# The bias keys' dot products with the query weights, moved from GpSimd and VectorE to TensorE

## What is computed

```python
qh = (q_in @ wq + bq).reshape(b, q_len, H, K)
kh = (kv_in @ wk + bk).reshape(b, t, H, K)
kh = jnp.concatenate([kh, jnp.broadcast_to(bias_k, (b, 1, H, K))], axis=1)
logits = jnp.einsum('bqhk,bthk->bhqt', qh, kh) / scale
```

## Time and profile before

| what | us |
|---|---|
| median of 3 runs | 1135.85 (1135.51 to 1137.48) |
| the profiled execution's own time | 1132.89 |
| its span in the trace | 1131.1 |
| TensorE matmul busy | 956.8 (85%) |
| TensorE weight loads busy | 809.0 (72%) |
| VectorE busy | 817.2 (72%) |
| ScalarE busy | 603.5 (53%) |
| GpSimd busy | 336.1 (30%) |
| mean granted TensorE clock | 0.929 of full |

### The profile page before, as it was taken

The page is one execution under the profiler, slowest core; times in us unless marked ns, Lnnn a source line. Parts: engine busy times, 40 slices in busy tenths (PEclk is TensorE's granted clock), DMA queues, the critical chain, the costliest instruction groups (busy, mean ns, idle before and its releaser), DMA issues. The chain is left out here.

```text
span 1131.1 us, 17854 instructions
## 1 busy us (share of the span) xinstructions
PE 956.8 (85%) x6548; PEld 809.0 (72%) x6548; DVE 817.2 (72%) x1624; ACT 603.5 (53%) x1367; POOL 336.1 (30%) x325
## 2 busy tenths in 40 slices
PE   4888886569999999997899999998586898478958
PEld 3666665558888889887778989987475566465647
DVE  3377767976787878787578787877664787757865
ACT  2488873034555555553355555655424786257842
POOL 4255541441112222221111222200005454534520
PEclk8889997888999999998899999999788799688989
DMA  5984106140001111111000111000305930296120
GB/s 180 252 130 63 12 1 247 56 162 1 15 24 38 38 39 38 38 38 39 1 4 36 38 38 38 2 1 1 117 1 123 169 44 1 59 191 73 13 80 19
DMA packets 37810, 69.49 MB, mean 61 GB/s; under 512 B 7414, under 2 KB 23288, under 8 KB 35036
## 3 DMA queue, kind: packets, MB, share of 16 engines
q1 hardware_dynamic: 37724, 68.35, 24.7%
HBM read 57.31 MB, written 11.02 MB: 60 GB/s over the span
## 5 line engine op out<-in xcount | busy, mean ns | idle before, releaser
L1230 ACT CAST L1a_probsT_hi<-L1a_bank 128x512 fp32r<-128x512 f32 x128 | 68.8, 589 | 94.3 <-PE L1a_bank L1111 94.3
L1069 POOL TENSOR_SCALAR L1a_wo_hi<-L1a_stage 128x512 fp32r<-128x512 f32 x16 | 10.3, 646 | 363.2 <-PE L1a_sums L74 355.6
L1347 DVE TENSOR_REDUCE L1a_top<-L1a_scores 128x2 f32<-128x1024 f32 x64 | 78.2, 1222 | 36.1 <-PE L1a_scores L74 36.1
L1262 ACT ACTIVATE L1a_probs<-L1a_scores,L1a_neg_max 128x512 f32<-128x512 f32 x128 | 86.8, 684 | 30.6 <-DVE L1a_bias_shifted L1351 25.6
L1285 DVE TENSOR_TENSOR L1a_probsT_lo<-L1a_bank,L1a_probsT_hi 128x512 fp32r<-128x512 f32 x128 | 82.0, 682 | 0.1
L72 PE MATMUL L1a_bank<-L1a_probsT_hi,L1a_v_hi 128*128 128x256 f32 x256 | 73.2, 286 | 9.2 <-DVE L1a_probsT_lo L1285 9.2
L1232 ACT ACTIVATE L1a_attended_hi<-L1a_bank,L1a_cols 128x256 fp32r<-128x256 f32 x64 | 30.5, 476 | 90.4 <-PE L1a_bank L74 90.4
L72 PE MATMUL L1a_bank<-L1a_w_hi,ctxT_hi 128*128 128x256 f32 x256 | 76.5, 299 | 1.1 <-DVE latT_lo L1303 1.0
L74 PE MATMUL L1a_bank<-L1a_w_hi,ctxT_lo 128*128 128x256 f32 x256 | 73.7, 288 | 0.0
L73 PE MATMUL L1a_bank<-L1a_w_lo,ctxT_hi 128*128 128x256 f32 x256 | 73.6, 288 | 0.0
L390 POOL TENSOR_SCALAR L0a_probs<-L0a_probs,L0a_inverse 128x768 f32<-128x768 f32 x64 | 57.2, 906 | 52.9 <-DVE L0a_inverse L641 52.9
(11 more groups left out here) (409 smaller groups left out, 3160.8 us busy)
## 6 DMA issues: line engine op xcount, KB each, us to landing
L1a_stage<-in_L_w SPq DMA_DIRECT2D x15, 1024.0 KB, 4.8
L0m_fold_wq<-in_L_wq SPq DMA_DIRECT2D x2, 2048.0 KB, 19.8
L0a_k_stack<-L0a_k_dram SPq DMA_DIRECT2D x12, 192.0 KB
L0a_w_qkv<-L0a_k_dram SPq DMA_DIRECT2D x12, 192.0 KB
L0a_probs<-in_L_wo SPq DMA_DIRECT2D x1, 2048.0 KB, 9.7
L0a_probsT<-in_L_wo SPq DMA_DIRECT2D x1, 2048.0 KB, 11.2
L0m_stage<-in_L_wm SPq DMA_DIRECT2D x4, 512.0 KB, 5.8
L0m_fold_bias_k<-in_L_bias_k SPq DMA_DIRECT2D x2, 1024.0 KB, 15.4
```

What stands on the lines that cost most here:

```text
L1230: nc.scalar.copy(out, source).then_inc(ring.hi_done, 1)
L1262: nc.scalar.activation(probs[:, g % 2, qt, :], scores[:, qt, :], ACT.Exp, bias=neg_max[:, g % 2, qt:qt + 1], accum_out=row_sum[:, g % 2, q ...
L1347: link(nc.vector.tensor_reduce(top[:, :], scores[:, :, :], AX.X, ALU.max))
```

## The change

GpSimd's three multiplies, VectorE's one and its four reductions are gone, and so is the broadcast load of `bias_k`. The query weights are now handed in transposed, `L1_wqT` [128, 16, 256]: the 128 columns of a head lie on the partitions. In their place TensorE makes 64 fp32 matmuls, one for each attention, half of the 256 input rows, and head: the stationary side is a 128 x 128 piece of the transposed weights, the moving side one column, the head's `bias_k` (from `L1_cols`, 32 KB, loaded in place of the broadcast). Each gives one column of a bank. This is one more job of the ring, `fold_job`, between the last up job and the first down job; the down jobs take the next bank each. ScalarE copies the 128 x 64 result to `folded`.

```diff
--- before.py
+++ after.py
@@ -777,7 +777,8 @@
         w2 = [t[:, 4:8, :].rearrange("p s (g n) -> p (s g) n", g=2) for t in w]
         rows = keep[cfg["rows"]]
         up0 = KT
-        down0 = up0 + FT + (len(context.jobs) if cfg["context"] else 0)
+        fold_job = up0 + FT
+        down0 = up0 + FT + (len(context.jobs) if cfg["context"] else 0) + (1 if fold else 0)
 
         @block.sync
         def _(sp):
@@ -800,8 +801,6 @@
         @block.gpsimd
         def _(pool):
             parts.root(nc, pool)
-            if fold:
-                fold.multiply(nc, pool, nc.gpsimd, fold.pieces[:3])
             if cfg["context"]:
                 context.root(nc, pool)
 
@@ -821,6 +820,9 @@
                 last.then_inc(ring.full, 1)
             if cfg["context"]:
                 context.transpose(nc, pe, ring, keep)
+            if fold:
+                ring.wait_bank(pe, fold_job)
+                fold.multiply(nc, pe, ring.bank(fold_job)).then_inc(ring.full, 1)
             pe.wait_ge(w_lo, 8)
             for t in range(RT):
                 job = down0 + t
@@ -850,6 +852,10 @@
                                      bias=b1[:, m:m + 1]).then_inc(ring.hi_done, 1)
             if cfg["context"]:
                 context.scale(nc, act, ring)
+            if fold:
+                act.wait_ge(ring.full, fold_job + 1)
+                nc.scalar.copy(keep["folded"][:, :, :, :].rearrange("p i k h -> p (i k h)"),
+                               ring.bank(fold_job)[:, 0:2 * KT * H]).then_inc(ring.freed_by(fold_job), 1)
 
         @block.vector
         def _(dve):
@@ -874,17 +880,11 @@
                     context_link = Chain(dve, context.dve_done)
                     dve.wait_ge(context_loaded, 16)
                     context.statistics(nc, context_link, context_rows, 1e-5, True)
-                if fold and m >= FT - 2:
-                    fold.reduce(nc, dve, keep, *fold.pieces[m - FT + 2])
                 if cfg["context"] and m == 3:
                     context.apply(nc, dve, context_rows, True)
             if cfg["context"]:
                 context.split(nc, dve, context_link, ring, cfg["context"])
-            if fold:
-                fold.multiply(nc, dve, nc.vector, fold.pieces[3:])
             for t in range(RT):
-                if fold and t < 2:
-                    fold.reduce(nc, dve, keep, *fold.pieces[3 - t])
                 job = down0 + t
                 dve.wait_ge(ring.full, job + 1)
                 nc.vector.tensor_tensor(keep["x"][:, t, :], ring.bank(job)[:, 0:D], keep["x"][:, t, :],
@@ -895,29 +895,26 @@
 
 
 
+
     def __init__(self, ph):
-        self.wq = [ph.sb(f"fold_wq{i}", [P, KT, H * DW]) for i in range(2)]
-        self.bias_k = [ph.sb(f"fold_bias_k{i}", [P, H * DW]) for i in range(2)]
+        self.wq = [ph.sb(f"fold_wq{i}", [P, H, D]) for i in range(2)]
+        self.cols = [ph.sb(f"fold_cols{i}", [P, 4, H]) for i in range(2)]
         self.loaded = [ph.sem(f"fold_loaded{i}") for i in range(2)]
-        self.multiplied = [[ph.sem(f"fold_multiplied{i}{kt}") for kt in range(KT)] for i in range(2)]
-        self.pieces = [(i, kt) for i in range(2) for kt in range(KT)]
 
     def load(self, sp, io):
         for i in range(2):
-            sp.dma_start(self.bias_k[i][:, :], io[f"L1_bias_k{i + 1}"].partition_broadcast(P)).then_inc(self.loaded[i], 16)
-            sp.dma_start(self.wq[i][:, :, :], io[f"L1_wq{i + 1}"].rearrange("(k p) n -> p k n", p=P)).then_inc(self.loaded[i], 16)
-
-    def multiply(self, nc, engine, on, pieces):
-
-        for i, kt in pieces:
-            engine.wait_ge(self.loaded[i], 32)
-            on.tensor_tensor(self.wq[i][:, kt, :], self.wq[i][:, kt, :], self.bias_k[i][:, :],
-                             ALU.mult).then_inc(self.multiplied[i][kt], 1)
-
-    def reduce(self, nc, dve, keep, i, kt):
-        dve.wait_ge(self.multiplied[i][kt], 1)
-        nc.vector.tensor_reduce(keep["folded"][:, i, kt, :], self.wq[i][:, kt, :].rearrange("p (h d) -> p h d", h=H),
-                                AX.X, ALU.add)
+            sp.dma_start(self.cols[i][:, :, :], io[f"L1_cols{i + 1}"]).then_inc(self.loaded[i], 16)
+            sp.dma_start(self.wq[i][:, :, :], io[f"L1_wqT{i + 1}"]).then_inc(self.loaded[i], 16)
+
+    def multiply(self, nc, pe, bank):
+        for i in range(2):
+            pe.wait_ge(self.loaded[i], 32)
+            for kt in range(KT):
+                for h in range(H):
+                    at = (i * KT + kt) * H + h
+                    last = nc.tensor.matmul(bank[:, at:at + 1], self.wq[i][:, h, kt * P:(kt + 1) * P],
+                                            self.cols[i][:, 1, h:h + 1], start=True, stop=True)
+        return last
 
 
 def wide_attentions(nc, io, keep):
@@ -1460,7 +1457,7 @@
         by_pair = [tiles(w).reshape(P, KT, PAIRS, 2 * DW).transpose(2, 0, 1, 3).reshape(PAIRS, P, -1) for w in (wq, wk, wv)]
         by_pair.append(wo.reshape(PAIRS, 2, P, D).transpose(0, 2, 1, 3).reshape(PAIRS, P, -1))
         t[f"L1_w{n}"] = np.concatenate(by_pair, axis=2)
-        t[f"L1_wq{n}"], t[f"L1_wo{n}"], t[f"L1_bias_k{n}"] = wq, wo, a[f"L1_xattn_bias_k{n}"].reshape(-1)
+        t[f"L1_wqT{n}"], t[f"L1_wo{n}"] = wq.reshape(D, H, DW).transpose(2, 1, 0), wo
         t[f"L1_cols{n}"] = np.stack([columns(a[f"L1_xattn_{m}{n}"].reshape(-1)) for m in ("bq", "bias_k", "bv", "bias_v")], axis=1)
         t[f"L1_bk{n}"], t[f"L1_bo{n}"] = columns(a[f"L1_xattn_bk{n}"]), a[f"L1_xattn_bo{n}"]
 
```

## The result

| | median us | runs | ratio to before, 95% interval |
|---|---|---|---|
| before | 1135.68 | 4 (1135.48 to 1137.48) | 1 |
| after | 1147.78 | 4 (1144.72 to 1152.1) | 1.011 (1.0086 to 1.0134) |
| after, once more, later (`e11_after`) | 1149.25 | 6 (1144.75 to 1151.42) | 1.0126 (1.0098 to 1.0155) |

The changed kernel is slower by 12.1 us, in the later comparison by 15.2 us (before was at 1134.04 there). The forecast was +12.65 us. The profiled execution of after is the slowest of its four, 1152.1 us with a span of 1150.3, so its trace holds some 4 us that the median doesn't. The four runs of before lie within 2 us; the 24 runs of before beside the first experiments cover 1126.90 to 1145.69 us, so a median of a few runs is good to some microseconds only.

What follows compares the result with a forecast made beforehand. L0m was taken to be bound by TensorE waiting for VectorE, which GpSimd's multiplies slowed. Terms: -13.55 + 24.4 + 1.8 = +12.65 us, median 1148.5 us; own range 1146 to 1151, for 8 in 10 1136 to 1152.

Steps and rivals of the forecast that it cites:

- What bounds L0m before, and what is removed: L0m: TensorE's waits for VectorE vanish, returning 11.75 us ahead of the down jobs and 1.8 us in them, 13.55 in all.
- The cost of a pair: Fold in L0m: each weight load and matmul, bound by its load, takes 0.112 us at 2.4 GHz, 0.213 at 1.2 GHz.
- That the clock falls in a busy TensorE: Fold in L0m: the clock drops to 1.2 GHz without TensorE idling, so 99 of 128 pairs run slow; fold 24.4 us.
- When it falls: Fold in L0m: full clock lasts 3.3 us, 29 pairs, chosen from earlier falls after 2.5, 3.3 and 4.0 us.
- The cold start of the down jobs: L0m's down jobs begin at 1.2 GHz for 4.0 us, losing 1.8 us (1.2 to 2.2).
- ScalarE's copy, the data: L0m: the copy beside the down jobs costs nothing; data land at 197.9, ahead of the fold's start at 201.24.
- L0m in all: The whole predicted change, all of it in L0m: -13.55 + 24.4 + 1.8 = +12.65 us.
- Nothing is moved in L1a: L1a, the phase behind L0m: starts with the barrier, cold as before, and waits for its own load; no change.
- (1): Rival for the fold: the clock holds at full speed; +0.8 us, 1136.6 us; chance 0.10.
- (2): Rival for the fold: the clock falls but loads don't slow, 0.112 us a pair; +2.6 us, 1138.5 us; chance 0.06.
- (3): Rival for the fold: two pairs share one load, 64 loads in place of 128; -6.4 us, 1129.5 us; chance 0.05.
- (4): Rival for the fold: loads at 1.2 GHz don't overlap with the matmul before, up to 0.33 us; up to +25 us; chance 0.04.

Runs made afterwards that it cites:

- e11_after: The changed kernel as it is, run again later beside the other kernels; 1149.25 us, 1.0126 of before.
- e1_none: Changed kernel without the fold's 64 matmuls and ScalarE's copy, data still loaded, GpSimd setting `folded` to zero; 1124.29 us, 0.9908 of before.
- e3_wide64: Changed kernel with each fold matmul streaming 64 columns in place of one, the further ones filler; 1132.24 us, 0.9981 of before.
- e2_twice: Changed kernel with the fold's 64 matmuls issued twice into the same columns; 1174.62 us, 1.0353 of before.
- e4_wide16: Changed kernel with each fold matmul streaming 16 columns in place of one, the further ones filler; 1146.11 us, 1.0086 of before.
- e10_quiet_after: Changed kernel, with GpSimd in L1a starting its splits of later weights only when VectorE is done with `latT`; 1139.05 us, 1.0028 of before.
- e7_hold: Kernel before, with GpSimd's three multiplies held until VectorE has freed the last up job's bank; 1130.27 us, 0.9952 of before.

## Why the prediction was right, and where it was not

**What bounds L0m before, and what is removed: right.** -13.55 us was predicted, `e1_none` has -14.2. Part of the difference is the clock's return, 3.7 us behind the first up job there and 5.0 us before. The up jobs run without a gap. In after, the first up job starts at 189.10 and the fold at 202.91, 13.8 us, where the prediction's 187.69 to 201.24 is 13.55. The down part without disturbance was put at 12.0 us; `e1_none` shows 213.78 - 201.81 = 12.0.

**The cost of a pair: right at both clocks.** 0.112 us at 2.4 GHz (`e3_wide64`), 0.211 at 1.2 GHz (`e2_twice`), where 0.112 and 0.213 had been taken. The value at 1.2 GHz had no row and could have been 0.112 or 0.33; to double the part bound by the load was the right choice. Its working was looser than its result: twice 0.109 is 0.218, not 0.213, and the load's duration grew by 0.145 us (188 to 333 ns) while the distance of two pairs grew by 0.099 only. The Trainium skill, page "TensorE: Matmul & The Clock Gate", section "LDWEIGHTS (loading the stationary operand)", gives one time for 128 columns, 107 ns, with no term for the clock. The distance of 0.112 us at full clock is near it; the 0.211 us at half speak against it, and so does the load's own 333 ns.

**That the clock falls in a busy TensorE: right, and now shown** by 64 columns against 16 and one. The two short stretches of 16-column matmuls in the old trace did tell it. The rule of the same page, section "Why this matters for your kernels", that TensorE must have no idle gaps, would have left the clock up; TensorE had none here, and the clock fell in five of five traces with the fold in one piece of 1 or 16 columns.

**When it falls: the term that was mis-sized.** "I take 3.3 us, the second, in the middle: 29 pairs." Measured were 5.5 us in after, 5.1 in `e2_twice`, 4.8 in `e4_wide16`, 4.8 in `e10_quiet_after` and 4.6 in `e11_after`, all above the 2.5 to 4.0 us that the old falls gave. In those I had counted from the first 16-column matmul; why the falls came sooner there is open. In after 5.5 us hold 49 pairs, so the fold took 225.10 - 202.91 = 22.2 us and not 24.4; in `e11_after`, with the earlier fall, its loads span 23.3 us.

**The cold start of the down jobs: right.** 3.8 us against 4.0; from 225.10 to 238.83 they took 13.7 us, predicted 12.0 + 1.8 = 13.8. ScalarE's copy, the data (in SBUF at about 198.3, 197.9 predicted) and the bank cost nothing, as said: no wait stands ahead of the fold or of the down jobs.

**L0m in all** came out at +10.5 us (after) and +11.5 (`e11_after`), not +12.65, by the later fall.

**"Nothing is moved in L1a": the step that failed.** The instructions are the same, but their meeting is not: whether VectorE or GpSimd comes first is decided by less than a microsecond, and 3.8 and 3.9 us were added in the two traces of the changed kernel as it is. The rows that would have warned me stood in the old trace, a cast of 3.32 us where others take 0.42. I read L1a for its small matmuls alone. So that the medians of +12.1 and +15.2 us lie near +12.65 is in part luck: two errors of opposite sign, -1 to -2 us in L0m and up to +4 us in L1a. The error in L1a by itself would have led past the upper end of the forecast's own range (1148.5 + 3.8 = 1152.3 us, against 1151).

The rivals: the clock did not hold (1), it did not leave the loads alone (2), there were 128 loads and not 64 (3), and at 1.2 GHz they overlapped, starting 0.21 us apart with 333 ns each (4).

## What to carry to other kernels

Cost small matmuls by their weight loads, and ask what they stream: here a run of one-column or 16-column matmuls halved the clock under a TensorE that never stopped, so put them between wide ones, or let them stream filler (8 us of 22 came back here for nothing). Before moving work off two engines that disturb each other, try moving it in time: holding GpSimd's multiplies until the banks were free (`e7_hold`) was worth 0.5%, the move to TensorE cost 1.1%. And when a change shifts a phase, look in the next ones for VectorE instructions that last many times their usual; here they marked a race that a shift of less than a microsecond turned over.

## What the runs showed of the hardware that I had not expected

**A VectorE cast or two-input instruction that begins beside a GpSimd instruction waits for the end of it.** Four additions that began beside GpSimd's splits took 6.62 us in seven of the traces and 6.63 in an eighth, one GpSimd instruction each, and 1.43 us without them. A cast that began in the midst of a GpSimd instruction ended 0.29 us behind it. It goes by which comes first: in `e7_hold` the two-input multiply on VectorE began 0.16 us ahead of GpSimd's first and took its usual 2.29 us, to 205.86. Then it was GpSimd that waited. VectorE's three reductions that need GpSimd's multiplies start at 210.38, 214.90 and 219.36, so GpSimd's second and third took 4.5 us each, and its first, from 203.73 on, about 6.6, which is 4.5 from 205.86 on. It goes by the kind, too: reductions, and adds with one input from a bank, were never stretched. The Trainium skill, page "SBUF — State Buffer", section "Who interferes with whom", says that the pair of ports that the two engines share is locked for a whole instruction by whoever comes first: against a VectorE cast in one of its two-port modes, against one with two inputs in SBUF while GpSimd's reads SBUF, and on this chip never against a reduction. These rows agree; which mode the casts ran in no row names.

**More work can be faster.** 64 columns in each of the fold's matmuls in place of one took L0m from 54.7 to 45.2 us and the kernel from 1.011 to 0.998 of before. No run has a number between 16 and 64.
